# A graph layer's second preparation: the row of own scores by way of memory instead of a product on TensorE

## The reference

```python
h = jnp.maximum(_layernorm(x, axis=-1), 0.0)
Wh = h @ W                      # (8192, 128)
s1 = Wh @ a1                    # one "own" score a row
s2 = Wh @ a2                    # one "neighbour" score a row
e = leaky_relu(s1[:, None] + s2[None, :], negative_slope=0.2)
attention = softmax(where(adj > 0, e, -9e15), axis=1)
x = x + elu(attention @ Wh)
```

## Time and profile before

| | |
|---|---|
| median of 3 runs | 1359.65 us (1357.86 to 1359.94) |
| the profiled execution | 1364.51 us, of which the span of instructions 1362.7 us |
| busy: PE, DVE, ACT, POOL | 1270.7, 1043.8, 980.1, 165.8 us |
| PE, share of the span | 93% |
| mean granted TensorE clock | 0.979 of 2.4 GHz |

### The profile page before, as it was taken

One profiled execution on the slowest core, in us unless ns is written; L12 is line 12 of the kernel. 1 busy time (PEld: TensorE's weight loads), 2 busy tenths in 40 slices (PEclk: granted clock), 3 DMA queues, 4 the chain that ended last, 5 costly groups with the idle time before them and its releaser, 6 DMA issues.

```text
span 1362.7 us, 74732 instructions
## 1 busy us (share of the span) xinstructions
PE 1270.7 (93%) x31691; PEld 1125.0 (83%) x31691; DVE 1043.8 (77%) x2196; ACT 980.1 (72%) x2100; POOL 165.8 (12%) x331
## 2 busy tenths in 40 slices
PE   4868899999999999999999999988899999999996
PEld 3657788888888888888888888876899989999996
DVE  6846467767776766777777677657899989999997
ACT  4855466666666666666666666667898989999995
POOL 4210111111111111111111111012000000000000
PEclk9969899999999999999999999999899999999998
DMA  9773699999999999999999999610234334334332
GB/s 188 77 89 67 91 127 138 139 138 129 140 140 131 133 137 133 136 137 141 129 138 141 140 126 139 108 48 2 73 111 117 100 102 127 108 100 126 112 96 73
DMA packets 103503, 157.54 MB, mean 116 GB/s; under 512 B 11456, under 2 KB 36288, under 8 KB 102848
## 3 DMA queue, kind: packets, MB, share of 16 engines
q0 software_dynamic: 36864, 67.13, 52.4%
q1 hardware_dynamic: 66496, 88.37, 20.0%
HBM read 314.84 MB, written 41.94 MB: 262 GB/s over the span
## 4 chain that ended last, share of the span: by engine, by line
PE 76%; issue 9%; ACT 8%; DVE 4%; DMA 2%; POOL 1%; ACTq 0%; SPq 0%; DVEq 0%; POOLq 0%
PE ps L883 16%; PE ps L787 16%; PE ps L734 10%; PE ps L857 9%; PE ps L766 6%; PE ps L749 4%; PE ps L761 4%; PE ps L722 4%; ACT arena L1117 3%; ACT arena L1126 3%; PE ps L775 1%; DMA arena<-in_adjB 1%; PE ps L663 1%; PE ps L639 1%; PE ps L880 1%
## 5 line engine op out<-in xcount | busy, mean ns | idle before, releaser
L787 PE MATMUL ps<-arena 128*128 128x129 f32 x2048 | 246.6, 279 | 0.0
L883 PE MATMUL ps<-arena 128*128 128x129 f32 x2048 | 244.9, 278 | 0.7 <-issue 0.7
L1133 ACT ACTIVATE arena<-ps,neg_max 128x1024 f32<-128x1024 f32 x128 | 142.3, 1112 | 135.5 <-PE ps L787 135.5
L787 PEld LDWEIGHTS ps<-arena 128*128 128x128 f32 x2048 | 237.8, 194 | 0.0
L883 PEld LDWEIGHTS ps<-arena 128*128 128x128 f32 x2048 | 236.7, 194 | 0.9 <-issue 0.9
L1486 DVE TENSOR_REDUCE mx<-ps 128x1 f32<-128x1024 f32 x128 | 156.7, 1225 | 97.1 <-PE ps L766 92.7
L1117 ACT ACTIVATE arena<-ps 128x512 f32<-128x512 f32 x256 | 152.6, 596 | 100.9 <-PE ps L734 100.9
L589 POOL DMA_DIRECT2D arena<-in_adjB x256 | 136.6, 534 | 688.2 <-PE ps L749 672.6
L1691 DVE TENSOR_SCALAR arena<-arena 128x128 f32<-128x128 f32 x768 | 202.6, 341 | 15.0 <-issue 8.6
L1111 ACT ACTIVATE arena<-ps 128x512 f16<-128x512 f32 x256 | 153.6, 600 | 41.2 <-PE ps L722 38.6
L734 PE MATMUL ps<-arena 128*32 128x128 f16 x8192 | 164.7, 222 | 19.0 <-issue 9.3
(11 more groups left out here) (164 smaller groups left out, 1321.8 us busy)
## 6 DMA issues: line engine op xcount, KB each, us to landing
arena<-in_adjB POOLq DMA_DIRECT2D x256, 256.0 KB, 8.1
sel_pick<-arena SPq DMA_DIRECT2D x64, 256.0 KB, 6.2
sel<-arena SPq DMA_DIRECT2D x64, 256.0 KB, 6.2
arena<-sel_pick SPq DMA_DIRECT2D x64, 256.0 KB, 3.5
arena<-sel SPq DMA_DIRECT2D x64, 256.0 KB, 2.7
arena<-in_xB SPq DMA_DIRECT2D x4, 1024.0 KB, 6.0
x_t<-in_x SPq DMA_DIRECT2D x64, 64.0 KB, 5.0
x_mid<-arena SPq DMA_DIRECT2D x64, 64.0 KB, 5.1
```

Source lines behind the costliest of these rows:

```text
L787: last = nc.tensor.matmul(pv_ps, p_T[:, s * P:(s + 1) * P], v_sel[:, b, s, :], start=False, stop=(s == SB - 1), skip_group_check=True)
L883: last = nc.tensor.matmul(xv_ps[b], w_msk[:, b, s, :], x1_sel[:, b, s, 0:VW], start=False, stop=(s == SB - 1), skip_group_check=True)
```

## The change

`project` of the second preparation no longer makes the row product, and does not wait for the last tile of layer one at its second group. `read_scores` takes exp of the own score's column of the four-tile product instead (4 columns on 128 partitions) into a small table `r_cols` of 64 columns. SP, after it has loaded the selection of tiles 0 and 1, stores that table in four quarters to a new row `r_all` in memory, 2048 single numbers to a quarter, waits until the quarter has landed, and loads it back over all 128 partitions into `r_row` (1 MB to a quarter). `weights` and `bend` wait for their quarter at tiles 0, 16, 32 and 48. `decide` no longer waits for the row.

```diff
@@ project, transposes @@
                 elif mode == 1:
-                    nc.tensor.matmul(row_ps[b], wa_rep[:, 0, :], hT, start=True, stop=True)
                     for i in range(NGRP):
...
                 for b in range(2):
-                    if mode == 1 and b == 1:
-                        pe.wait_ge(y_ready, TILES)
                     project(b, b, base, mode)
@@ read_scores @@
-                nc.scalar.activation(r_row[:, bass.ts(G, GW)], row_ps[b], ACT.Exp, scale=SLOPE - 1.0
+                nc.scalar.activation(r_cols[:, bass.ts(G, NGRP)], vs_ps[b][:, :, D], ACT.Exp, scale=SLOPE - 1.0
                                      ).then_inc(row_ready, 1)
@@ SP @@
+            def spread_rows(q):
+
+                part_of = slice(q * N // 4, (q + 1) * N // 4)
+                sp.wait_ge(row_ready, 4 * q + 4)
+                with nc.allow_non_contiguous_dma(reason="2048 numbers"):
+                    sp.dma_start(r_all[0:1, part_of].rearrange("o (t p) -> p (o t)", p=P), r_cols[:, 16 * q:16 * q + 16]
+                                 ).then_inc(r_out[q], 16)
+                sp.wait_ge(r_out[q], 16)
+                sp.dma_start(r_row[:, part_of], r_all[0:1, part_of].to_broadcast([P, N // 4])).then_inc(r_in[q], 16)
...
             for t in range(2):
                 load_selection(t, t)
+            for q in range(4):
+                spread_rows(q)
@@ bend (ACT), and the same in weights (DVE) @@
+                if t % 16 == 0:
+                    act.wait_ge(r_in[t // 16], 16)
                 own = r_row[:, bass.ts(t, P)]
@@ decide (DVE) @@
                 dve.wait_ge(proj_lo, 2 * PREP)
-                dve.wait_ge(row_ready, PREP)
                 dve.wait_ge(lengths_ready, 1)
```

More of the change, by code:

```diff
@@ L45, with gnn_kernel @@
 TOP_LIMIT = float(2 ** 50)
-def gnn_kernel(nc, x, xB, adj, adjB, Ws, Wt, Wc, W1, a1, out, x_mid, sel, sel_pick):
+def gnn_kernel(nc, x, xB, adj, adjB, Ws, Wt, Wc, W1, a1, out, x_mid, sel, sel_pick, r_all):
     N = x.shape[0]
@@ L122, in gnn_kernel @@
         assert W1A + 6144 <= TOP + 2304 and 5120 + 2048 <= VALS
+        r_cols = part(MASK + 8 * XW + 2 * P, TILES)
         m_in = part(MASK + 2048, 1024, F16).rearrange("p (r n) -> p r n", r=2)
@@ L195, in gnn_kernel @@
         vs_ps = [ps[:, 2 * b:2 * b + 2, :].rearrange("p h (i c) -> p (h i) c", c=GW // 2)[:, :, 0:D + 2] for b in range(2)]
-        row_ps = [ps[:, 6 + b, :] for b in range(2)]
         v_ps = [ac_ps[:, b, :] for b in range(2)]
@@ L240, in gnn_kernel @@
         row_ready = sem("row_ready")
+        r_out = [sem(f"r_out{q}") for q in range(4)]
+        r_in = [sem(f"r_in{q}") for q in range(4)]
         lengths_ready = sem("lengths_ready")
@@ L1683, in weights @@
                 dve.wait_ge(m_ld[b], (t - b) * 8 + 16)
+                if t % 16 == 0:
+                    dve.wait_ge(r_in[t // 16], 16)
                 own = r_row[:, bass.ts(t, P)]
@@ L1971 @@
     sel_pick = nc.dram_tensor("sel_pick", (shape[0] // P, P, 1024), _mybir.dt.float16, kind="Internal").ap()
-    gnn_kernel(nc, *args, out, x_mid, sel, sel_pick)
+    r_all = nc.dram_tensor("r_all", (1, shape[0]), _mybir.dt.float32, kind="Internal").ap()
+    gnn_kernel(nc, *args, out, x_mid, sel, sel_pick, r_all)
     r = _run(nc, [arrays], core_ids=[0])
```

## The result

| | median (lowest to highest, runs) | ratio to before, 95% interval |
|---|---|---|
| before | 1358.76 us (1356.62 to 1359.94, 4) | |
| changed | 1373.67 us (1372.68 to 1374.64, 4) | 1.0112 [1.0094, 1.0129] |

The change makes the kernel 14.9 us slower, outside the range of 1352.8 to 1362.0; the forecast was 1355.3. The profiled execution took 1373.13 us, with a span of 1371.1.

The account below looks back on a forecast made before the run. It took PE's chain of products and turnings, 2.355 us a group, to bound the second preparation, with ACT's 2.20 next. Gains of 0.44 + 2.06 + 1.86 = 4.36 us from the median 1359.65 gave 1355.3 us, range 1352.8 to 1362.0.

Parts of the forecast that it names:

- the landing of the store: SP's store of each quarter to memory: lands 5.6 us after issue, so SP keeps up with releases every 8.8 us.
- the bounds of 2.3 and 27 us: Store landing on SP: below, the 256 KB end store's 2.3 us; above, 27 us if `a_sb`'s 3.4 went with count.
- From 8.9 us on: Landing time at which SP's four store waits start to delay the load for tile 2; each us more costs four.
- the 4.36 us of gain: Whole second preparation: 0.44 ahead, 2.06 steady and 1.86 tail, ending near 946.4 us.
- the rival: SP's way through memory doesn't keep up, delaying the load for tile 2; slower, chance 0.20.
- L = 11: Rival's case of a store landing in 11 us: PE waits 8.5 us at tile 2, time 1363.8 us.
- the reason for the pace before: Second preparation: row product, four-tile product and turnings, all on PE, set the pace of 2.355 us a group.
- Ahead: Start of the second preparation on ACT: the first exp becomes a small one, gaining 0.44 us.
- From there to the end of the last turning: Steady part, group 5's rows to group 15's turnings: ACT's loop of 2.20 us a group, 25.63 to 23.57, gain 2.06.
- The tail: From the last turning to the preparation's end: 6.73 us before, T + 4.87 after, gain 1.86 us.
- No clock was lost: Rival: PE's clock falls to 1.2 GHz in the relieved preparation, costing 4.5 us, so no change, 1359.8; chance 0.06.
- the rival of lost time: Around the decision, half clock or the last 1 MB of reading gives back 2 to 3 us: 1357.5; chance 0.16.

Follow-up runs that it names:

- e5: Against e3, nine stores of different patterns on SP behind the preparation, each waited for; 1404.03 us, one run.
- e6: e3 with one normalised row tile of four on ACT and three on POOL from group 2 on; 1350.09 us, one run.
- e4: The changed kernel with the row product and its wait for layer one's last tile back on PE; 1373.17 us, ratio to before 1.0098.
- e3: The changed kernel without the way through memory, layer two's weights made from a constant tile; 1357.77 us, ratio to before 0.9988.
- e1: The changed kernel with three of SP's four waits and loads back moved into layer two; 1370.04 us, ratio to before 1.0078.
- e9: The changed kernel with each quarter turned on PE, so SP stores 16 rows of 512 bytes; 1359.24 us, ratio to before 0.9992.
- e10: e9 with one row tile of four on ACT and three on POOL from group 2 on; 1355.32 us, ratio to before 0.9962.
- e11: e3 plus the four stores of adjacent single numbers, not waited for until layer two's second eighth; 1361.53 us, one run.
- e12: e3 plus the four stores, numbers 64 bytes apart, not waited for until layer two's second eighth; 1359.42 us, one run.
- e2: The changed kernel storing runs of 64 bytes, with readers taking every 16th number; 1379.91 us, ratio to before 1.0153.

## Why the prediction was wrong

**The step that failed is the landing of the store.** The prediction took "the store's row: four times the packets; if 1.1 of its 2.3 us go with their number, 4 x 1.1 + 1.2 = 5.6 us". Measured were 12.3 to 13.7 us. It treated the cost as one of count, took it from a store in packets of 512 bytes, and set aside `a_sb`'s, the only row of single numbers. e5 shows that the count matters little (128 numbers take 7.81 us, 2048 take 10.44). And no division of the 2.3 us by count could have come out right: with all of it going with the number, four times the packets make 9.2. The true value lay between the bounds of 2.3 and 27 us. From 8.9 us on, by the prediction's own working, each us costs four, so the 4.36 us of gain are used up at 10.0, and most of the interval is beyond that. A chance of 0.20 for the rival was too little.

**The rival was right as a mechanism.** It put the first release 9.2 us behind the first load, and it was 9.20 (912.71 - 903.51). Its formula, 912.71 + 4 x (13.1 + 0.45) with the mean of the four landings, gives 966.9 us for SP to be free, and it was at 966.60. Its price at L = 11, 1363.8, with four for each us more is 1372.2 at 13.1; measured were 1373.67. What it lacked is the gap in PE's instructions and the late signal to ACT (1.63 and 2.57 us in the timeline of the result) and tile 2 at half clock.

**The preparation was right term by term, and the reason for the pace before was wrong.** Ahead, to the rows of group 5, the changed kernel needs 8.25 us where before needs 8.70: 0.45 less, forecast 0.44. From there to the end of the last turning it is 23.58 in place of 25.63: 2.05, forecast 2.06. The tail is 2.10 shorter, forecast 1.86.

```profile
911.76 0.86 ACT L992 ACTIVATE arena<-arena,rstd 128x128 f32<-128x128 f32 x2
...
934.68 0.66 PE L653 MATMUL ps<-ident,arena 128*128 128x128 f32 x4 [0.65 <-ACT arena L992]
```

PE waits for ACT's rows, as the prediction said, and e6 shows that this loop sets the 2.20. No clock was lost in it (0.98). This isn't luck: the times of before were measured, and those of after are the loops of the earlier trace rows. But the chain of the earlier trace rows was read as PE's own work, and it wasn't: the pace was that of the round over two buffers, in which PE's product, ACT's row exp and DVE's splitting follow one another. The chain itself has a product that takes less than the 0.96 to 1.10 us of the reading, and with 0.89 and 0.45 it gives the 2.20 of e4:

```profile
929.98 0.86 PE ps L663 x2
```

e4 has the product, its wait for layer one and the small exp, and 38.37 us. Taken in this order, 2.72 of the 4.60 come from the end of the row exp, and 1.88 from the product and its wait; no run takes these two apart. The last group shows the rest of the round in the changed kernel:

```profile
936.72 1.13 PE L678 MATMUL ps<-w_scores,arena 128*128 128x130 f32 x8 [0.49 <-DVE arena L1442]
...
939.28 0.69 DVE L1442 TENSOR_TENSOR arena<-ps,arena 128x512 f16<-128x512 f32 x1
```

From the wait for DVE to DVE's last operation it is 3.25 us there, and 4.51 at the same place before, 946.24 to 950.75.

**Around the decision** the rival of lost time had a small part: +0.31 us, with 48 gathers ahead of the bounds at 1.51 us in place of 0.95. The clock is at half from their start in the changed kernel (0.50), and 0.86 for them before. More isn't lost there without the stores: up to tile 23 e3 is no later than before.

## What to carry to other kernels

Ask of a store of single numbers not how many they are but whether numbers of different partitions lie side by side in memory. If they do, turn the table first (one product for each quarter here): the store then lands in 1.3 to 3.8 us instead of 12.3 to 13.7.

A chain of waits on one queue has a number at which it stops keeping up. Where the unknown cost may lie on either side of it, the chance belongs to the interval and not to the value that looks most natural.

When a chain of waits runs on one engine without a gap, look whether its buffers go around through the others. Here the exchange of two instructions on ACT made the preparation 2.18 us shorter; the whole change, which takes away the product (0.86 of PE's 2.20 us a group) and ACT's row exp, made it 4.60 shorter.

## What the runs showed of the hardware

- A store of 2048 adjacent single numbers lands 12.3 to 13.7 us after its issue, although all its packets are through after 2.3 us (changed kernel). With nothing else on its queue it takes 10.4 to 10.8 (e5); the first one of e1, with another in flight, takes 14.7. 64 bytes apart the same numbers take 4.4 (e5), and turned into 16 rows of 512 bytes 1.3 to 3.8 (e9, e10).
- With such stores in flight, engines wait up to 4.9 us for signals that no engine shown releases (e5, 950.03), and the decision takes 7.3 to 8.3 us in place of 5.1 in e1, e5 and e11. It stays at 5.08 in the changed kernel and e4, where the late signals come behind it. With the stores 64 bytes apart nothing of the kind is seen (e12, 5.09).
- A step of 64 bytes in the operand of a 128x128 operation: 347 to 412 ns on DVE, 496 to 612 on ACT (e2 against the changed kernel).
